# Two waits of a graph kernel made fewer: row buffers freed by the products' own count, and one bank wait for eight tiles

## The reference, cut to what matters

```python
ft = (feat @ W_fc).reshape(N, H, D)
e = jax.nn.leaky_relu(eh[src] + ee + et[dst], negative_slope=NEG_SLOPE)
...
ex = jnp.exp(e - e_max[dst])
a = ex / denom[dst]
msg = ft[src] * a[:, :, None]
rst = jax.ops.segment_sum(msg, dst, num_segments=N)
...
msgs = feat_src[src]
sums = jax.ops.segment_sum(msgs, dst, num_segments=n)
```

## Time and profile before

| what | value |
|---|---|
| median of 3 runs | 4067.09 us (4066.4 to 4073.57) |
| the profiled execution | 4042.07 us |
| its span, first to last instruction | 4040.4 us |
| attention's products (L1138) | 559 to 1757 us of the span |
| second sum's products (L1396) | 2335 to 3467 us of the span |
| busy in the span: PE, DVE, ACT, POOL | 61%, 50%, 32%, 45% |
| granted TensorE clock, mean | 0.705 |

### The profile page before, as it was taken

The page is one execution under the profiler, slowest core; times in us unless marked ns, Lnnn a source line. Parts: engine busy times, 40 slices in busy tenths (PEclk is TensorE's granted clock), DMA queues, the critical chain, the costliest instruction groups (busy, mean ns, idle before and its releaser), DMA issues. The chain is left out here.

```text
span 4040.4 us, 51661 instructions
## 1 busy us (share of the span) xinstructions
PE 2474.9 (61%) x12916; PEld 2128.5 (53%) x12916; DVE 2006.0 (50%) x6407; ACT 1290.8 (32%) x4654; POOL 1799.1 (45%) x1888
## 2 busy tenths in 40 slices
PE   6964636666666666655899944545545445646348
PEld 5853525555555555544677634544444444535347
DVE  7930247777777777745645432322323223354325
ACT  2311123334334344442233222323323223352113
POOL 0043156666666666403100066666666666241255
PEclk9966666667766776767888856666666666756579
DMA  6343323333333333345000033333333333330043
GB/s 182 100 102 85 120 70 91 91 91 90 89 89 91 91 91 90 76 116 164 20 21 21 18 90 92 90 93 90 93 93 90 93 90 92 103 94 1 25 127 94
DMA packets 262938, 348.49 MB, mean 86 GB/s; under 512 B 153465, under 2 KB 193519, under 8 KB 261143
## 3 DMA queue, kind: packets, MB, share of 16 engines
q0 software_dynamic: 87936, 235.05, 20.8%
q1 hardware_dynamic: 174726, 110.32, 10.7%
HBM read 288.25 MB, written 61.20 MB: 86 GB/s over the span
## 5 line engine op out<-in xcount | busy, mean ns | idle before, releaser
L1376 POOL DMA_INDIRECT Gb<-normed_rows,SRCT x784 | 743.3, 948 | 741.4 <-SPq L1368 358.7
L1396 PE MATMUL pAb<-HOTb,Gb 128*128 128x128 f32 x3136 | 580.5, 336 | 564.0 <-issue 551.2
L1396 PEld LDWEIGHTS pAb<-HOTb,Gb 128*128 128x128 f32 x3136 | 524.2, 247 | 620.6 <-issue 603.5
L1438 DVE TENSOR_TENSOR ACC<-ACC,pAb 128x256 f32 x784 | 330.7, 422 | 800.1 <-DMA sums_by_rank<-rrowa 576.4
L981 POOL DMA_INDIRECT GX<-ft_rows,SRCT x560 | 532.2, 950 | 355.5 <-PEq L1144 211.7
L1138 PE MATMUL apA<-AHOT,GX 128*128 128x129 f32 x2368 | 481.8, 385 | 220.0 <-DVE GX L1278 195.6
L1138 PEld LDWEIGHTS apA<-AHOT,GX 128*128 128x128 f32 x2368 | 449.9, 292 | 255.7 <-DVE GX L1278 223.6
L1066 ACT ACTIVATE ACC<-apA 128x254 f32 x784 | 301.0, 384 | 694.6 <-PE apA L1138 299.1
L1415 ACT ACTIVATE HOTb<-OFFb 128x1024 f32<-128x1024 f32 x98 | 103.6, 1057 | 769.8 <-DMA sums_by_rank<-rrowa 757.5
L1411 ACT ACTIVATE OFFb<-iota,NRELb 128x128 f32<-128x128 f32 x784 | 239.8, 388 | 6.7
L981 POOL DMA_INDIRECT G<-ft_rows,SRCT x192 | 183.2, 954 | 111.0 <-PEq L1144 62.2
(11 more groups left out here) (386 smaller groups left out, 4615.9 us busy)
## 6 DMA issues: line engine op xcount, KB each, us to landing
ebuf<-in_edge_attr_dram SPq DMA_DIRECT2D x49, 448.0 KB
Gb<-normed_rows,SRCT POOLq DMA_INDIRECT x784
rows_by_expert<-ffn_PADT SPq DMA_DIRECT2D x1, 10360.0 KB
sT<-rows_by_expert SPq DMA_DIRECT2D x80, 129.5 KB
GX<-ft_rows,SRCT POOLq DMA_INDIRECT x592
sums_by_rank<-rrowa SPq DMA_DIRECT2D x49, 128.0 KB, 1.7
sums_by_rank<-rrowb SPq DMA_DIRECT2D x49, 128.0 KB, 1.7
GX<-in_x_dram SPq DMA_DIRECT2D x11, 560.0 KB
```

The source lines that it names most:

```text
L1376: pool.indirect_dma_start(G[g % R][m][:, :], None, TABLE[:, :], bass.IndirectOffsetOnAxis(ap=SRCT[:, t:t + 1], axis=0)).then_inc(g_in[g % ...
L1396: last = nc.tensor.matmul(pA[b][:, o:o + EP], G[k][m][:, c * 128:(c + 1) * 128], HOT[k % 2][:, m, :], start=True, stop=True)
L1438: last = nc.vector.tensor_tensor(acc[:, :, ds(b, EP)], acc[:, :, ds(b, EP)], pA[q][:, o:o + KD * EP].rearrange("p (c r) -> p c r", c=KD), ...
```

## The change

In the attention the semaphore g_free goes. PE no longer waits for its own product after every fourth tile, and raises nothing there; POOL waits for the count of the quarter's last product, prod of bank 3, in its place. In the second sum PE no longer waits for each bank before its two tiles; from the third group on it waits once, at the group's start, for the last bank of the group before last, and DVE raises pfree once a group, after its eighth addition, where it did so after every second. The increments that set the semaphores off at the start of either stage go too.

```diff
@@ attend
-        g_free, pre_free, acc_zero = sem("arows_free"), sem("pre_free"), sem("acc_zeroed")
+        pre_free, acc_zero = sem("pre_free"), sem("acc_zeroed")
...
-                        pool.wait_ge(g_free, c * WG + m // WB + 1)
+                        pool.wait_ge(prod[NBK - 1], (c - GS) * CPB + m // NBK + 1)
...
-                pe.sem_inc(g_free, GS * WG)
...
-                        if m % WB == WB - 1:
-
-                            pe.wait_ge(prod[b], c * CPB + m // NBK + 1)
-                            pe.sem_inc(g_free, 1)
@@ sum_segments
                     pe.wait_ge(hot[k % 2], r * 2 + k // 2 + 1)
+
+                    if g >= 2:
+                        pe.wait_ge(pfree[last_bank(k)], r * 2 + k // 2)
...
-                        if m % 2 == 0:
-                            pe.wait_ge(pfree[b], r * 2 + k // 2 + 1)
...
-                for m in range(K):
-                    dve.sem_inc(pfree[m], 1)
...
-                        if m % 2:
+                        if m == K - 1:
                             last.then_inc(pfree[q], 1)
```

## The result

The changed kernel takes 4058.37 us (median of 9 runs, 4048.93 to 4064.87) where the kernel before took 4071.92 us (9 runs, 4066.4 to 4082.15). The ratio is 0.9961, 95% interval 0.9947 to 0.9975: faster by 0.39%, 10 to 22 us. I had forecast 4063 us, a gain of 4 us, and called "no change" the likeliest.

What follows compares the result with a forecast made beforehand. POOL's gather issues and PE signals arriving some 1.7 us after POOL stops were taken to bound both loops. Relay -4 us, self-wait 0, second sum 0, off the median 4067.09, gave 4063 us; range 4042 to 4118.

Steps and rivals of the forecast that it cites:

- Fewer waits: Second sum: PE's bank waits go from four a group to one, DVE's increments likewise; priced at 0.
- coarser wait: Second sum: PE waits for all of the group before last, ending a group 1.2 us later; 5 us spare, priced 0.
- slower rival: Second sum: late group-end signals make POOL stop after eight issues; +45 us, or +138 if always; chance 0.30.
- The relay: Attention: POOL waits for the product's count directly, not PE's increment at L1144; 0.09 us over 45 rounds, 4 us.
- PE's wait for itself: Attention: dropping it brings product L1105 earlier, but DVE's next start hangs on POOL's stop; costed at 0.
- that cover: Attention: DVE's next start follows POOL's stop, so an earlier transpose of scores only waits longer.
- DVE's 41 us: Attention: DVE's wait for PE's product L1105; rival that it comes off the end, 4022 us, chance 0.10.
- DVE's wait ahead of L1265 shrinks, the one ahead of L1181 grows by as much: Attention sign: time DVE saves at the first wait returns at its wait for the transpose of scores.
- L1181 comes without its wait: Attention, sign of error: DVE would go on without the late transpose signal, forecast 1.7 us after POOL's burst.
- The bursts of L1376: Second sum, sign of error: POOL's gather bursts would become shorter or longer than 16.
- The third quarters' duration: Attention, sign of error: the time of PE's third quarter, 3.63 us in the loop, would move.
- TensorE's clock: Rival: the clock falls otherwise, third quarters shorter or longer, 16 us either way; chance 0.06 faster, 0.03 slower.

Runs made afterwards that it cites:

- f2: Only the second sum's half of the change, attention as before, against the kernel before on a chip of 4080 us: 0.9997.
- h1: The whole change plus repeated POOL wait instructions between gathers of both stages, against the kernel before: 1.0018.
- f1: Only the attention's half, relay and PE's self-waits both gone, against the kernel before: 4056.52 against 4080.03 us, 0.9941.
- f3: Only the relay removed, PE's wait for its own product every fourth tile kept, against the kernel before on a chip of 4080 us: 0.9982.
- g2: The attention's half, but PE waits for its own product after every second tile, against the kernel before: 4193.96 against 4081.31 us, 1.0272.
- g3: The attention's half, but PE waits for its own product once, after a round's last tile, against the kernel before: 4068.73 against 4081.31 us, 0.9964.
- e1: Only the attention's half, second sum as before, against the kernel before on the chip of 3580 us: 0.9993.
- e3: Only the relay removed, PE's self-wait kept, against the kernel before on the chip of 3580 us: 3568.26 us, 0.9963, five runs.
- e4: The whole change again, against the kernel before on the chip of 3580 us: 0.9988.
- e2: Only the second sum's half, attention as before, against the kernel before on the chip of 3580 us: 1.0003.

## Why the prediction was right and wrong

**The number: partly luck.** The 4063 us lie 5 us from the measured 4058.37, but I had taken 4 us off a median of three runs (4067.09). Nine runs gave 4071.92, so the gain was 13.6 us, more than three times mine and beyond the 8 us that I had called no change. "Faster" had 0.24 in all.

**The second sum: right.** Fewer waits 0, coarser wait 0. The half measured 0.9997 on one chip and 1.0003 on the other. Bursts stayed at 16 and the restarts 23.16 us apart. PE was two rows further back and not five or six. My slower rival (bursts of eight, 0.30) didn't come in the two profiles that have this half alone or in the whole change on such a chip (after, f2). It came in part in h1, with wait instructions between the gathers, and there its price was too high: some 10 us for 21 stops more.

**The relay: right.** I took 0.09 us on the loop, 4 us in all, bounds 2 and 6. The restart came 0.09 us sooner (medians 0.36 and 0.27); the timed kernel was 7 us faster, with an interval (2 to 13 us) that holds the 4.

**PE's wait for itself: the step that failed.** I costed it at 0, "with that cover gone it is worth up to 41 us", because DVE's next start hangs on POOL's stop and an earlier transpose only waits longer. f1 against f3 gives 16 us on the same chip, four times the gain that I forecast in all. Two things were missing from the step. First, I read only DVE's 41 us; the waits of PE ahead of L1105 were in the profile too, 28.4 us for its own product and 10.8 "remote", and the latter are late signals like the transposes': POOL's bursts delay PE's signal to itself as well (g2 shows it, 3.1 us in one round). Second, the cover is not complete. Rounds exist in which the transpose's signal comes through after 0.5 us, behind a short stop of POOL, and in these profiles they appear only without the self-wait: four in after, three in f1, nine in h1, none in before, f2, f3, g2 or g3. But they give back most of what they gain in the next round (at most 1 us is left of each pair), so they explain some 3 of the 16 us. How the rest reaches the end stays open: the profiles of f3 and f1 differ in DVE's two waits, U_f and BU, by 6 us (185.4 + 62.2 against 190.2 + 51.4) and in their 45 rounds by 2 us, and one execution each can't carry more. On the chip of 3580 us no gain of this kind was measured, rather the reverse (e1 0.9993, e3 0.9963).

**DVE's wait ahead of L1265 shrinks, the one ahead of L1181 grows by as much: not settled.** Before against after says no: the first stayed (45.6 and 48.6), because the earlier product's signal is late in its turn, and the second fell from 195.6 to 186.5. The three profiles of the one chip say yes: from f2 over f3 to f1 the first goes 96.9, 62.2, 51.4 and the second 152.5, 185.4, 190.2. They are single executions, and the same code gave 45.6 and 96.9.

**The signs of an error.** "L1181 comes without its wait" was one, and it came, in four rounds. The bursts of L1376 stayed at 16. The third quarters' duration did not move (3.47 us before and 3.44 after, means of 44 rounds).

**TensorE's clock.** I had thought that an attention without self-waits might keep a higher clock, and gave it 0.06. The rows point the other way where they differ at all: 0.75 (e1, e4) against 0.78 and 0.77 (e2, e3) on the chip of 3580 us. That would explain why e3 beats e1 and e4 there, but I have not shown it.

**No faster version for all chips.** On the chip of 3580 us the best of the kernels is e3, PE's self-wait kept and only the relay removed (0.9963, five runs). On the chip of 4080 us it is f1 (0.9941), the attention's half, though the whole change was not timed beside it. Nothing there says that the second sum's half should be kept for the time.

## What to carry to other kernels

Ask for each signal what is being issued while it travels: on the chips of 4080 us a wait that looks free cost 3 us where it fell into an unbroken row of gathers (g2), and 0.30 us where POOL stood still. What a wait costs is its place, not its instruction. Before costing a self-wait at nothing, look in the profile at what the engine waits for behind it, not only at the next engine. And where a gain hangs on such delays, time it on more than one chip: the same change was worth 0.39% on one and nothing that could be measured on another.

## What was not expected of the hardware

The same program takes 3580 us on one chip and 4067 to 4081 on others; 29 runs of the kernel before on the one lay between 3571 and 3627 us, 62 on others between 4066 and 4095. On the faster one POOL issues all 784 gathers of the second sum in a row, 1.25 us apart, and no wait in the profiles of e1 to e4 is put to "remote". On the others signals of PE and of DVE are late while gathers are issued without a break. In all 45 such rounds of the kernel before DVE goes on 1.5 to 1.8 us after POOL's last issue, and in 40 of 41 of the kernel after 1.7 to 1.9 us. Not every signal is late: in the four rounds of the kernel after it is raised two or three gathers behind a short stop, and comes through in 0.5 us. These two stages are not the whole difference between the chips: the attention's products start at 481 to 485 us of the span on the faster one, and at 559 before. The DMA issues of the page differ as well (KB or none, then the median us from issue to landing); e2, on the faster chip:

```profile
Gb<-normed_rows,SRCT POOLq DMA_INDIRECT x784, 2.7
```

and f2, the same code on another, for which the page gives no landing:

```profile
Gb<-normed_rows,SRCT POOLq DMA_INDIRECT x784
```

That the gathers' own arrival signals crowd out the others there is a guess, and the two kernels that were to test it by the pace of the issues did not change the pace as meant. A drain of POOL behind a gather took 3.0 us. Two or three wait instructions between gathers left the issues 1.25 us apart, but the kernel with them was 7 us slower than the one before and not faster.
